# Gated linear attention and feed-forward layer: dt moved into the decays' exponent, scores as three products of rounded halves, the halves of the queries turning over in one buffer

## The reference

```python
dt = softplus(h @ Win.T + dt_bias);  g = -dt * exp(A_log_bias)
G = cumsum(g, axis=-1)                       # within a chunk of 128
scores = einsum('bhnid,bhnjd->bhnij', qc, kc)          # q and k after rope
decay = where(causal, exp(G[:, None] - G[None, :]), 0)
y_intra = einsum('bhnij,bhnjd->bhnid', scores * decay, v * dt)
cstates = einsum('bhnjd,bhnje->bhnde', kc * exp(Glast - G), v * dt)
y_inter = einsum('bhnid,bhnde->bhnie', qc * exp(G), state_of_the_chunk_before)
y = rmsnorm(y_intra + y_inter) * gnorm_w * silu(h @ Wg.T)
out = y @ Wo.T
```

## Time and profile before

| | |
|---|---|
| median of 3 runs | 1065.32 us (1064.6 to 1066.32) |
| the profiled execution: its own time, its span | 1066.14 us, 1064.4 us |
| granted TensorE clock, mean | 0.994 |
| busy share of the span | PE 97%, PEld 76%, DVE 74%, ACT 66%, POOL 20% |
| chain that ended last | PE 89%, DVE 3%, DMA 3%, issue 2%, ACT 2% |

### The profile page before, as it was taken

The page is one execution under the profiler, slowest core; times in us unless marked ns, Lnnn a source line. Parts: engine busy times, 40 slices in busy tenths (PEclk is TensorE's granted clock), DMA queues, the critical chain, the costliest instruction groups (busy, mean ns, idle before and its releaser), DMA issues.

```text
span 1064.4 us, 14465 instructions
## 1 busy us (share of the span) xinstructions
PE 1030.6 (97%) x4678; PEld 804.4 (76%) x4678; DVE 785.5 (74%) x1543; ACT 707.6 (66%) x1373; POOL 215.1 (20%) x132
## 2 busy tenths in 40 slices
PE   5989999999999999999999999999999798999998
PEld 3767777777777777777777777777777467888786
DVE  6668887887888888878887887888887885334322
ACT  3457877877788788878877877788777655233300
POOL 2212221211222221112121211212223520000000
PEclk8999999999999999999999999999999999999999
DMA  8432411220131013102411220131032303111011
GB/s 312 139 144 65 129 26 40 79 79 20 39 118 39 20 39 118 39 20 65 126 26 39 79 79 20 39 118 39 20 99 60 99 21 128 60 40 60 20 40 40
DMA packets 37947, 74.09 MB, mean 70 GB/s; under 512 B 3264, under 2 KB 19936, under 8 KB 35616
## 3 DMA queue, kind: packets, MB, share of 16 engines
q1 hardware_dynamic: 37056, 73.30, 21.6%
q10 hardware_dynamic: 864, 0.43, 0.1%
HBM read 69.38 MB, written 2.24 MB: 67 GB/s over the span
## 4 chain that ended last, share of the span: by engine, by line
PE 89%; DVE 3%; DMA 3%; issue 2%; ACT 2%; POOL 1%; SPq 0%; DVEq 0%; ACTq 0%; POOLq 0%
PE ps_q_gt L68 14%; PE ps_q_gt L70 14%; PE ps_q_gt L69 14%; PE ps_ss_o L68 5%; PE ps_ss_o L70 5%; PE ps_ss_o L69 5%; PE ps_s_y L798 5%; PE ps_kv_x L70 3%; PE ps_kv_x L69 3%; PE ps_kv_x L68 3%; PE ps_s_y L807 2%; PE ps_kv_x L821 2%; PE ps_s_y L68 2%; PE ps_s_y L69 2%; PE ps_s_y L70 2%
## 5 line engine op out<-in xcount | busy, mean ns | idle before, releaser
L1861 POOL TENSOR_TENSOR q_sin<-q_sin,cst 128x512 f32<-128x512 f32 x64 | 89.5, 1398 | 304.8 <-ACT q_sin L1001 304.8
L1575 DVE SCALAR_TENSOR_TENSOR prob<-ps_s_y,scal,dec 128x128 f32<-128x128 f32 x252 | 70.8, 343 | 76.7 <-PE ps_s_y L798 76.7
L68 PE MATMUL ps_q_gt<-hT_hi,wq_hi 128*128 128x512 f32 x256 | 124.7, 487 | 1.2 <-DVE q_cos L1385 1.2
L1849 POOL TENSOR_TENSOR dec<-dec,future 128x1024 f32<-128x1024 f32 x31 | 74.4, 2401 | 248.6 <-ACT expg L1020 248.6
L68 PE MATMUL ps_ss_o<-wo_hi,z_hi 128*128 128x512 f32 x260 | 103.7, 399 | 1.6 <-DVE z_lo L63 1.6
L68 PE MATMUL ps_q_gt<-hT_hi,wg_hi 128*128 128x512 f32 x256 | 103.6, 405 | 0.0
L70 PE MATMUL ps_ss_o<-wo_hi,z_lo 128*128 128x512 f32 x260 | 102.5, 394 | 0.0
L69 PE MATMUL ps_ss_o<-wo_lo,z_hi 128*128 128x512 f32 x260 | 102.3, 394 | 0.0
L69 PE MATMUL ps_q_gt<-hT_lo,wg_hi 128*128 128x512 f32 x256 | 101.1, 395 | 0.0
L70 PE MATMUL ps_q_gt<-hT_hi,wg_lo 128*128 128x512 f32 x256 | 100.8, 394 | 0.0
L70 PE MATMUL ps_q_gt<-hT_hi,wq_lo 128*128 128x512 f32 x256 | 100.5, 393 | 0.0
(11 more groups left out here) (272 smaller groups left out, 2613.1 us busy)
## 6 DMA issues: line engine op xcount, KB each, us to landing
dec<-gT_dram SPq DMA_DIRECT2D x32, 512.0 KB, 5.6
raw_q<-wq_in SPq DMA_DIRECT2D x32, 256.0 KB, 2.7
raw_g<-wg_in SPq DMA_DIRECT2D x32, 256.0 KB, 2.9
raw_o<-wo_in SPq DMA_DIRECT2D x8, 1024.0 KB, 7.0
raw_pair<-wkv_in SPq DMA_DIRECT2D x8, 512.0 KB, 4.5
raw_pair<-wgu_in SPq DMA_DIRECT2D x7, 512.0 KB, 3.3
raw_gu<-wgu_in SPq DMA_DIRECT2D x6, 512.0 KB, 3.3
x<-x_in SPq DMA_DIRECT2D x2, 1024.0 KB, 9.9
```

Source lines behind the costliest of these rows:

```text
L68: pe.matmul(out, w_hi, x_hi, start=first, stop=False)
L1575: last = nc.vector.scalar_tensor_tensor(prob[:, h], ps_s[:, h * P:(h + 1) * P], scal[:, tile, 1, h:h + 1], dec[:, tile // 2 % 2, h, tile % ...
L1849: nc.gpsimd.tensor_tensor(cells, cells, future[:].unsqueeze(1).broadcast_to([P, GRP * CPB, CHUNK]), ALU.add).then_inc(mask_done, 1)
L1861: nc.gpsimd.tensor_tensor(q2, q2, sinT, ALU.mult).then_inc(qsin_done, 1)
```

## The change

1. **dt in the exponent.** The decays become exp(G_i - G_j + ln dt_j). ScalarE takes one more logarithm ahead of the loop, VectorE one more addition (`decay_bias`), and dt is floored at 1e-20. `probabilities` no longer multiplies by dt for each head, so its four instructions become one `tensor_tensor` over 128x512. The table `scal` of scalars for each token loses a column.
2. **Scores in halves.** Queries and keys are kept as hi and lo (`q_hi`, `q_lo`, `kT_hi`, `kT_lo`), and `scores` and `cross_scores` are three fp32r products. The tail of the last group keeps fp32 (`scores_late`, `cross_scores_late`, on `q_late` and `kT_late`). ScalarE gains `round_q`, VectorE `split_q_lo` in each step and `split_k_lo` in odd steps. `rotate_q_add` writes into q_cos instead of qT, and q_cos is free again when `split_q_lo` is done.
3. **One buffer for the halves.** q_hi and q_lo hold one half of the tokens each. The head written in step t takes the cells of the tile that step t has just used (`head_cells`, `tile_cells`). The scores of tiles 0 and 4 wait for the four `split_q_lo` of the steps before them, and the scores of every even tile for `split_k_lo`.
4. **The lists of the steps.** Weights of the next group are split in steps 2, 3, 4, 6 instead of 1 to 4. In odd steps VectorE has sum_squares ahead of rotate_q_cos and gated_y ahead of rotate_q_add; TensorE has k_turn ahead of the whole g_block; ScalarE has copy_kT ahead of round_squares. In even steps ScalarE copies v after z_hi. GpSimd masks in the odd step, behind rotate_q_sin, instead of in the even one.
5. **Small tensors** (statistics, gates) move into the space of sq_top.

```diff
@@ TensorE
             def scores(g, t):
 
                 b, c, half = t // 2, t % 2, t // 4
+                pe.wait_ge(klo_done, g * 4 + (b + 1))
+                pe.wait_ge(qlo_done, g * 8 + (4 * half + 4))
+                cut = slice(c * P, (c + 1) * P)
+                three_products(nc.tensor, ps_s.rearrange("p (h i) -> p h i", h=GRP),
+                               kT_hi[:, b % 2, cut], kT_lo[:, b % 2, cut], tile_cells(q_hi, t), tile_cells(q_lo, t),
+                               True, True).then_inc(s_ready, 1)
...
-                if project:
-                    g_block(g, t, 0, 2)
                 if c == 1 and next_batch:
                     k_turn(g, b)
                 if project:
-                    g_block(g, t, 2, KT)
+                    g_block(g, t, 0, KT)
@@ ScalarE
+            def round_q(g, t):
+                half, j = (t // 4 + 1) % 2, t % 4
+                act.wait_ge(rope_done, g * 8 + (t + 5))
+                nc.scalar.activation(head_cells(q_hi, half, j), q_cos[:].rearrange("p (t i) -> p t i", t=GRP),
+                                     ACT.Copy).then_inc(qhi_done, 1)
...
+                if c == 1:
+                    copy_kT(g, b, kT_hi if next_group or b == 0 else kT_late)
                 round_squares(g, t)
-                if c == 1:
-                    copy_kT(g, b)
+                if next_group:
+                    round_q(g, t)
                 decays(g, t + 1)
@@ VectorE
-                for h in range(GRP):
-                    last = nc.vector.scalar_tensor_tensor(
-                        prob[:, h], ps_s[:, h * P:(h + 1) * P], scal[:, tile, 1, h:h + 1],
-                        dec[:, tile // 2 % 2, h, tile % 2], ALU.mult, ALU.mult)
-                last.then_inc(prob_done, 1)
+                nc.vector.tensor_tensor(prob[:], ps_s.rearrange("p (h i) -> p h i", h=GRP),
+                                        dec[:, tile // 2 % 2, :, tile % 2], ALU.mult).then_inc(prob_done, 1)
...
+            def split_q_lo(g, t):
+                half, j = (t // 4 + 1) % 2, t % 4
+                dve.wait_ge(qhi_done, g * 8 + (t + 5))
+                split_lo(nc.vector, head_cells(q_lo, half, j), q_cos[:].rearrange("p (t i) -> p t i", t=GRP),
+                         head_cells(q_hi, half, j)).then_inc(qlo_done, 1)
+
+            def split_k_lo(g, b):
+                dve.wait_ge(kT_done, g * 4 + (b + 2))
+                split_lo(nc.vector, kT_lo[:, (b + 1) % 2], ps_kv[:, 0:CPB * P], kT_hi[:, (b + 1) % 2])\
+                    .then_inc(klo_done, 1)
@@ GpSimd
                 if t == 0:
                     split_late_o(g)
-                if c == 0 and next_batch:
+                if c == 1 and next_batch:
                     mask(g, b)
```

More of the change, by code:

```diff
@@ L219, in layer @@
         raw_kv, raw_o = raw_pair, sb("raw_o", [P, GRP, HID])
-        qT = sb("qT", [P, 2, GRP, HALF])
+        q_lo, q_hi = (sb(n, [P, GRP, HALF], F32R) for n in ("q_lo", "q_hi"))
+        q_late = over("q_late", [P, GRP, HALF], F32, place["q_hi"])
+        x_mid = over("x_mid", [P, GRP, HID], F32, place["q_lo"])
         sg = sb("sg", [P, 2, GRP, HALF])
         dec = sb("dec", [P, 2, GRP, CPB, CHUNK])
-        kT = sb("kT", [P, 2, CPB * CHUNK])
+        kT_hi, kT_lo = (sb(n, [P, 2, CPB * CHUNK], F32R) for n in ("kT_hi", "kT_lo"))
+        kT_late = over("kT_late", [P, 2, CPB * CHUNK], F32, place["kT_hi"])
         expg = sb("expg", [P, GRP, CHUNK])
-        scal = sb("scal", [P, NT, 3, GRP])
+        scal = sb("scal", [P, 2 * CPB, 2, GRP])
         kr = sb("kr", [P, CPB, D])
@@ L281, in layer @@
         x_again = [raw[:].rearrange("p k d -> p (k d)") for raw in (raw_q, raw_g)] \
-            + [qT[:, 0, i] for i in range(GRP)] + [sg[:, 0, i] for i in range(2)]
+            + [x_mid[:, i] for i in range(GRP)] + [sg[:, 0, i] for i in range(2)]
         v_late = over("v_late", [P, D], F32, place["sq_parts"])
@@ L294, in layer @@
                      ("wo_lo", 4), ("wo_hi", 4), ("dec", 20))}
-        qT_at, sg_at = ([place[n] + i * TILE for i in range(2 * GRP)] for n in ("qT", "sg"))
+        qT_at, sg_at = ([place[n] + i * TILE for i in range(2 * GRP)] for n in ("q_lo", "sg"))
         homes = [c for n in ("sig", "q_cos", "q_sin", "wkv_lo", "wkv_hi") for c in cells_of[n]] \
@@ L936, in _ @@
             g = KVH - 1
-            scores(g, 4)
-            cross_scores(g, 4)
+            scores_late(g, 4)
+            cross_scores_late(g, 4)
             pe.wait_ge(kv_split, KVH)
@@ L944, in _ @@
             pe.wait_ge(prob_done, g * 8 + 5)
-            scores(g, 5)
+            scores_late(g, 5)
             out_with_sum(g, 4)
@@ L958, in _ @@
             pe.wait_ge(prob_done, g * 8 + 7)
[L959 removed]
+            scores_late(g, 7)
             pe.wait_ge(zz_done, g * 8 + 6)
@@ L1107, in _ @@
             copy_kT(0, -1)
+            round_q(0, -4)
             sigmoid(0, -4)
@@ L1117, in _ @@
             copy_rows(5)
+            round_q(0, -3)
             swap(0, -2)
+            act.wait_ge(chain, CHAIN_G - 1)
+            nc.scalar.activation(zq, zs2, ACT.Ln).then_inc(exp_done, 1)
             copy_gT(0)
@@ L1125, in _ @@
             nc.scalar.activation(zs, zs, ACT.Exp).then_inc(exp_done, 1)
+            round_q(0, -2)
             sigmoid(0, -2)
@@ L1133, in _ @@
             exp_gate(0, -1)
+            round_q(0, -1)
             sigmoid(0, -1)
@@ L1371, in rotate_k @@
                     dve.wait_ge(rope_done, g * 8 + min(t + 4, NT))
+                if b >= 0 and not late:
+                    dve.wait_ge(qlo_done, g * 8 + (t + 4))
                 nc.vector.tensor_tensor(k_cos, ps_k[:, :, 0:D], cos_k, ALU.mult)
@@ L1379, in rotate_k, with rotate_q_cos @@
                     .then_inc(kr_done, 1)
-            def rotate_q_cos(g, t):
+            def rotate_q_cos(g, t, late=False):
                 if t % 2 == 1 or t == -4:
                     dve.wait_ge(kr_done, g * 4 + (max(t, -2) // 2 + 2))
+                if t > -4 and not late:
+                    dve.wait_ge(qlo_done, g * 8 + (t + 4))
                 dve.wait_ge(swap_done, g * 8 + (t + 5))
```

157 lines of the change are left out of this document (99 added, 58 removed).

## The result

The change makes the kernel slower: 1139.65 us (median of 4 runs, 1138.42 to 1141.5) against 1064.96 beside it, a ratio of 1.070 (95% interval 1.068 to 1.071). The forecast of 1111 had the side right, but it put the loss at 46 us where 74.7 were measured, and the time lies above its range of 1058 to 1121. The profiled execution took 1138.99 us on a span of 1137.2.

A forecast was written before the change was run, and what follows sets the result against it. TensorE's list of work was taken as the bound before. Odd steps +52.5, last group +2.4 and -1.1, even steps -9.6 and loop start +1.9 made +46.1 on a span of 1064.4, so 1111 us, range 1058 to 1121.

The forecast's parts named there:

- The mechanism: Odd steps: GpSimd's sin precedes kr, the mask follows and holds sq_sum to 9.65 us, so TensorE waits for VectorE.
- The odd step laid out: Times from the scores' start to q_lo's end at 13.0 us; odd steps of 12.45 to 13.5 against 11.14.
- TensorE waits: Odd steps: TensorE idle for 1.3 to 2.4 us, ended by sq_parts, kT_lo or q_lo.
- the price of a product: TensorE: one fp32r product of 128x512 takes 0.23 us, three 0.70, one fp32 product 0.86.
- even steps: Loop: even steps shorten by 0.32 us to 13.50, 30 of them giving -9.6 us.
- tail and feed-forward part: Behind the loop: the shorter prob of the tail gives 0 to -1 us, taken as 0.
- loop start: First scores also wait for the last head's round_q and q_lo, which ends at 78.0: +1.9 us.
- The loss on odd steps: Four odd steps of a group lose 2.4, 1.9, 1.3 and 1.9 us, 7.5 a group, +52.5 in seven.
- The gain of the three products: TensorE's scores and cross scores: 0.16 us less for each of 60 and 30 products, 14.4 us less.
- kr in ahead: Rival, odd steps: kr runs before the sin, the mask holds only the rotated query; 1080 (1068 to 1090), chance 0.21.
- Faster: Rival: mask and VectorE hardly hold each other in the new place; 1057 (1050 to 1061), chance 0.19.

The follow-up runs named there:

- fill: Changed kernel with eight more fp32r products on TensorE in each odd step of the first seven groups, before the sum of squares: 1124.98 us.
- after_shift: Changed kernel with small tensors allocated ahead of the projections' weights, as in shift, no instruction changed: 1131.31 us.
- full_scores: halves_2 with the loop's scores and cross scores as one fp32 product each instead of three fp32r ones: 1077.33 us against 1063.68.
- before_mask_odd_2: Kernel before the change with one line changed, GpSimd's mask moved to the odd step behind the sin: 1100.48 us, ratio 1.033.
- halves_2: Changed kernel with the mask cut in two instructions, one ahead of the odd step's sin, one in the next even step after z_lo: 1063.68 us.
- shift192: halves_2 with small tensors placed ahead of the weights, which start 192 bytes higher; no instruction changed: 1054.68 us.
- kr_first_2: Changed kernel with GpSimd waiting in odd steps for kr ahead of the sin, the mask still behind it: 1104.61 us.
- shift64: halves_2 with two small tensors placed ahead of the weights, which start 64 bytes higher: 1062.77 us.
- shift: halves_2 with three small tensors placed ahead of the weights, which start 1216 bytes higher; no instruction changed: 1056.25 us.
- shift32: halves_2 with one small tensor placed ahead of the weights, which start 32 bytes higher: 1065.97 us.

## Why the prediction missed

**The mechanism was right**, to a tenth of a microsecond up to the rotated query. The odd step laid out, against step 7 above (S = 391.46), from the ends of the rows:

| | forecast | measured |
|---|---|---|
| scores ready for prob | 0.90 | 0.89 |
| z_hi starts | 2.3 | 2.38 |
| the sin starts | 5.2 | 5.27 |
| kr is asked for | 5.4 | 5.49 |
| the mask ends | 9.1 | 9.12 |
| sq_sum ends | 9.65 | 9.66 |
| rotated query ends | 11.45 | 11.46 |
| sq_parts ends | 12.0 | 12.18 |
| q_lo ends | 13.0 | 13.23 |

The Trainium skill, page "SBUF — State Buffer", section "Who interferes with whom", says that a VectorE instruction with two SBUF inputs and a GpSimd one that reads SBUF shut each other out, and that issue order decides. By that rule, the trace agrees: kr ended 0.28 us after the sin and sq_sum 0.54 us after the mask, each begun inside that instruction.

**The term that was missing: the clock.** This is the step of the prediction that failed: "TensorE waits" was priced as idle time alone, and the products behind the wait at full clock. The second is the price of a product, taken from the kernel before. The span missed by 1137.2 - 1110.5 = 26.7 us. Of it:

| piece | how worked out | us |
|---|---|---|
| half clock | steps 0 and 2: (14.99 - 13.65 + 14.28 - 13.65) x 7, and 1.5 in the last group | 15.3 |
| even steps | 13.65 at full clock, forecast 13.50, x 28 | 4.2 |
| odd steps | 13.32, 13.29, 12.69, 13.30 against 13.5, 13.1, 12.45, 13.1, x 7 | 3.2 |
| tail and feed-forward part | from the last group's step 4 on, 239.7 against 236.8, forecast 0 | 2.9 |
| loop start, rest of the last group | 78.51 for 78.1, and some 0.3 | 0.7 |

They add up to 26.3 of the 26.7. fill shows that the empty stretches are the cause of the first piece: with work in them nine of the ten slow stretches were gone, and 14.7 us. The second and the fourth are mostly one cause: products that start 0.233 us apart instead of 0.227, because the new buffers moved the weights; after_shift gave back 8.3. Neither alone would have brought the time under 1121 (fill 1124.98, after_shift 1131.31). The prediction read 0.23 per product from the earlier trace rows and took it for a property of the product; that the change moves addresses was in the diff and not in the sum.

**The loss on odd steps** was short by 0.2 in steps 3, 5 and 7, in the last instructions: sq_parts ends 0.72 us after the rotated query and q_lo 1.05 after that, where the layout had 0.55 and 1.0. Step 1 was forecast 0.2 too long.

**The gain of the three products**, 14.4 from rows, is 13.65 in full_scores. The estimate by the page "FP8 and Floating Point Precision" of the Trainium skill, section "TensorE Precision Notes" (four passes, 19.4), isn't borne out here; the measurement decides. An fp32r product costs more (0.227 to 0.234) than a quarter of an fp32 one (0.86 / 4 = 0.215).

**kr in ahead** had a chance of 0.21 and did not come true: in all 30 odd steps of the loop the sin started 0.22 us ahead of kr, in the trace of the changed kernel, about as forecast. Forced, it gives 1104.6 and not 1080. **Faster** (0.19) rested on a mask that holds nothing, and before_mask_odd_2 shows that it holds sq_sum. Its 1057 lies between the two times that the change gives once the mask is out of the way (halves_2 1063.7, shift192 1054.7); which of them one gets hangs on the place of the weights, with which it did not reckon.

## What to carry to other kernels

Before moving a GpSimd instruction, write down which VectorE instructions with two SBUF operands run in its new place, and who waits behind them: here one moved line cost 35 us, and the same work cut in two and put in other places cost next to nothing. When a forecast says that TensorE will wait regularly, price the clock too, with its own range: here waits of 1.35 and 0.50 us led to 1.5 us more in the next step, behind step 7 though not behind step 3. When buffers change size, compare the addresses of the operands that the bound engine reads, since all its products may change a little.

## What the runs showed of the hardware

- After the change, the same waits of 1.35 + 0.50 us lowered the clock behind step 7 (0.50 in 407 to 409) in groups 0 to 6, and never behind step 3. Behind the 1.95 to 2.0 of step 1, step 2 was slow in groups 0, 3 and 6 alone. In after_shift, with 1.44 + 0.50, step 7 was followed by a slow step in six of seven groups and step 3 in one. What picks the place is open. With shorter waits the loop stayed at full clock: 0.62 + 0.50 and, in step 1, 1.23 to 1.29 (kr_first_2), and 0.65 to 1.05 (before_mask_odd_2).
- With two GpSimd instructions in a row, a VectorE one that asks during the first ran between them: kr, asked for during the sin, ended 0.28 us after the sin, in the first 0.32 us of the mask as recorded, and the mask took 2.59 us instead of 2.40. One that asks during the second waits: sq_sum, asked for 0.24 us after the mask's start, waited for all of it.
- fp32r products of 128x512 in the feed-forward part start 0.227 us apart where the weights' address leaves 224 by 256, and 0.233 to 0.234 where it leaves 32, 64 or 96. Other remainders were not tried. In these products only the weights moved: hT_hi and hT_lo stayed, and their addresses (212960 and 196576) leave 224 too.
- The moving operand counts as well. In out_product the weights stayed (wo_hi at 188384, wo_lo at 180192) and z_hi and z_lo moved: over 709 products the mean from start to start is 0.228 to 0.229 us where z_hi (at 160736) leaves 224 (shift64, shift192, shift), and 0.230 to 0.233 where it leaves 96, 160 or 192 (before, halves_2, shift32). Whether both operands have to leave 224, or the same, isn't shown.
